# GpSimd's gathers for the expert tiles without their pacing wait, and one weight residual moved behind the first gather

## The chip, the cores and the metric

The kernel runs on one core of a Trainium2 chip. The metric is the device time of one execution in microseconds (us). The five engines are written as the profile writes them: PE is TensorE (PEld its weight loads), DVE is VectorE, ACT is ScalarE, POOL is GpSimd, SP is SyncE. Each engine runs its own list of instructions in order, and they meet only at semaphores; SP carries most of the DMA issues.

## The reference, cut to what matters

```python
# x: (128, 32, 128) f32; cond_8: (128, 8) router logits
# layer 0: x1 = x + ternary_ffn(layernorm(base + LoRA(x)))
# layer 1, the stage this document is about:
rw = jax.nn.softmax(router_logits.astype(jnp.float32), axis=-1)
w, sel = jax.lax.top_k(rw, TOP_K)                       # 2 of 8 experts for each sequence
dense_w = jnp.zeros((B, E), x.dtype).at[jnp.arange(B)[:, None], sel].add(w)
def _gemma_mlp(x, gate_w, up_w, down_w):
    g = jnp.einsum('bsh,hi->bsi', x, gate_w)
    u = jnp.einsum('bsh,hi->bsi', x, up_w)
    return jnp.einsum('bsi,ih->bsh', jax.nn.gelu(g, approximate=True) * u, down_w)
out = sum_e dense_w[:, e] * _gemma_mlp(x, skill_gate[e], skill_up[e], skill_down[e])
out = out + _gemma_mlp(x, shared_gate, shared_up, shared_down)
# then a second, quantised gated FFN on out, and the residual
```

Batch row b is one sequence of 32 steps with 128 features. Each sequence goes through two of eight experts (hidden width 512) and through one shared expert.

## The kernel before

**Tiles and units.** The router's choice gives 256 (sequence, expert) pairs. They are laid into 20 tiles, each of one expert: 14 narrow tiles of 12 sequences (384 columns) and 6 wide ones of 16 (512 columns). The order is narrow, narrow, wide, repeated, with two narrow tiles at the end (`TILES`, `size(i)`). PE works each tile in two units, so there are units 0 to 39. Unit s is 12 matmuls of gate and up (`ps<-xg,Wr`). Behind each unit PE does the six down matmuls of the unit before: four on the high halves (`ps<-Hh,WT`) and two on the low halves (`ps<-Hl,WT`).

**Split operands.** Each f32 operand is carried as a rounded high part and a residual: `WD` slot 0 and slot 1 for the down weights, `Hh` and `Hl` for the hidden values. A residual is a subtraction of two SBUF tensors, `low(...)`: L746 on DVE, L1545 on POOL.

**POOL around the change.** `down_low(k)` (k = 0 to 7) makes the residual of expert k's down weights and raises `k_wdl`. `fetch(i)` gathers tile i's sequences out of `XT` into `xg[:, i % 4]`, one copy for each sequence (CAST rows of L1626). It works in two parts, the first 8 sequences and the rest, each with a register load of the sequence numbers (a TENSOR_LOAD) ahead. Its last copy raises `k_xg`, for which PE waits ahead of unit 2i. `fetch(0)` also waits for `d_xt` 8, the eighth low half of `XT`. From i = 4 on a fetch waits for `p_eu` to reach 2(i-4)+2, that is for PE to have read tile i-4 out of the same buffer. From i = 2 on each of its parts also waits for `d_ehl`, which DVE raises once for each unit's `Hl`: for 2i-3 ahead of the first part and for 2i-2 ahead of the second.

**DVE around the change.** In its loop over s it does: eight or six scatters `C<-ps,Wt,C` of an earlier tile, a register load (`colI`), `Hl` of unit s-1, and `HbS` (gelu times up) of unit s, which frees PE's banks.

**SP around the change.** `load_tile(i, ...)` moves tile i's gate and up weights (1 MB) from `wscr` into `Wr[:, i % 3]`. The raw down weights `wdr` were staged in the bytes that become `Wr[:, 0]` and `Wr[:, 1]`. So `load_tile(0)` waits for `k_wdl` 4 and `load_tile(1)` for `k_wdl` 8. PE waits for the load ahead of unit 2i. ACT's `down_weights(0)`, which copies tile 0's down weights from `WD` to `WT`, waits for `k_wdl` 8 as well.

Of the kernel before, what the change touches and what calls it, by code (L numbers as in the profile page):

```python
# [49 lines left out]
def program(nc, x, cond, Wb, bb, As, Bs, fw, gamma, beta, sg, su, sd, hg, hu, hd, wg, wu, wd, out):  # L50
    ctx = ExitStack()
    with ctx:
# [14 lines left out]
        def sem(name):  # L67
            return ctx.enter_context(nc.semaphore(name))
# [154 lines left out]
        k_xg, p_eg, p_eu, a_eg, d_eh, a_ehh, d_ehl, p_ed, d_ey = (  # L223
           
            sem(n) for n in ("k_xg", "p_eg", "p_eu", "a_eg", "d_eh", "a_ehh", "d_ehl", "p_ed", "d_ey"))
# [53 lines left out]
        def cols(j):  # L279
            return slice(512 * j, 512 * j + 512)  # L280
# [20 lines left out]
        def size(i):  # L301

            return 16 if TILES[i] < 16 else 12
# [1234 lines left out]
        def _(e):  # L1538
            w = Waits(e)
# [4 lines left out]
            def low(o_, a, hi):  # L1544
                return e.tensor_tensor(o_, a, hi.bitcast(F32), SUB)  # L1545
# [22 lines left out]
            for n in range(12):  # L1568
                i = n - 2
# [23 lines left out]
            def down_low(k):  # L1593
                w.wait_ge(a_wdh, k + 1)
                low(WD[:, 1, cols(k)], wdr[:, k, :], WD[:, 0, cols(k)]).then_inc(k_wdl, 1)
# [14 lines left out]
            def fetch(i):  # L1610
                w.wait_ge(d_ord, 1)
                w.wait_ge(a_q, 8)
                w.wait_ge(p_q, 8)
                w.wait_ge(d_xt, 8)
                if i >= XR:
                    w.wait_ge(p_eu, 2 * (i - XR) + 2)
                for a_, b_ in ((0, 8), (8, size(i))):

                    if i >= 2:
                        w.wait_ge(d_ehl, 2 * i - 3 + (a_ > 0))  # L1620
                    t = PT * TILES[i] + a_
                    regs = nc.values_load_multi_w_load_instructions(
                        ordI[0:1, t:t + b_ - a_], engines=(mybir.EngineType.Pool,), min_val=0, max_val=127,
                        skip_runtime_bounds_check_because=WHY)[1]
                    for s in range(a_, b_):
                        last = e.tensor_copy(xg[:, i % XR, :, T * s:T * s + T].rearrange("p a t -> p a t"),  # L1626
                                             XT[:, :, :, bass.ds(regs[s - a_], 1)].rearrange("p a t o -> p a (t o)"))
                last.then_inc(k_xg, 1)

            for k in (4, 5, 6):  # L1630
                down_low(k)
            fetch(0)
            down_low(7)
            for i in range(1, NM):
                fetch(i)

# [18 lines left out]
            for n_, step in enumerate(POOL_ORDER):  # L1655
# [3 lines left out]
                k = POOLED.index(p) if p in POOLED else None  # L1659
# [143 lines left out]
```

## Time and profile before

| | |
|---|---|
| median of 3 runs | 400.34 us (400.22 to 400.65) |
| the profiled execution's own time | 400.22 us |
| its span in the trace | 398.5 us |
| PE busy | 346.2 us, 87% of the span |
| DVE busy | 330.8 us, 83% |
| ACT busy | 263.0 us, 66% |
| POOL busy | 223.4 us, 56% |
| expert stage, units 0 to 39 | from 89.1 to about 229.9 us |

The 1.7 us between the profiled execution's time and its span lie outside the trace. The busy shares are means over stages of different kind, so they don't say what bounds the expert stage. That is read from PE's idle gaps in that stage and from what ends each of them.

### The profile page before, as it was taken

The page shows a single profiled execution, that of the slowest core. Times are in us where ns is not written, and L with a number is a line of the kernel's source. Part 1 is how long each engine was busy: PE and PEld are TensorE (multiplying, and loading weights), DVE is VectorE, ACT ScalarE, POOL GpSimd, SP SyncE. Part 2 cuts the span into 40 slices and gives each one's busy share as a digit, 9 for nine tenths or more (in the row PEclk, how much of TensorE's full clock was granted, in tenths as well). Part 3 has the DMA queues.
Part 4 walks back from the last instruction along what each step waited for, and adds up shares of the span by engine and source line. Part 5 has one row for each costly group of instructions (what it writes and reads, how often), then busy time and mean ns, then how long its engine had stood idle before and what let it go on. Part 6 is the DMA issues. An engine that isn't in the chain of part 4 may idle for free.

```text
span 398.5 us, 6226 instructions
## 1 busy us (share of the span) xinstructions
PE 346.2 (87%) x1754; PEld 285.0 (72%) x1754; DVE 330.8 (83%) x700; ACT 263.0 (66%) x339; POOL 223.4 (56%) x400
## 2 busy tenths in 40 slices
PE   8979967999999999999999989999999971005997
PEld 7657744768898989989898977777677650003897
DVE  4588558975999999999999989765689899979894
ACT  3655687866576565666656544555467899999650
POOL 2656885897466473847465023222195568992462
PEclk9998999999999999999999999999999996555999
DMA  6998993955353443535332005100000000000022
GB/s 173 341 398 301 326 314 118 315 161 212 112 202 111 151 168 117 201 106 187 132 127 84 3 2 160 51 2 0 1 2 0 1 0 1 0 0 2 0 108 105
DMA packets 19850, 47.77 MB, mean 120 GB/s; under 512 B 2787, under 2 KB 8934, under 8 KB 17254
## 3 DMA queue, kind: packets, MB, share of 16 engines
q1 hardware_dynamic: 18342, 47.16, 33.8%
q10 hardware_dynamic: 1472, 0.20, 0.3%
q8 instruction: 14, 0.23, 0.2%
q14 instruction: 22, 0.18, 0.1%
HBM read 33.10 MB, written 12.58 MB: 115 GB/s over the span
## 4 chain that ended last, share of the span: by engine, by line
PE 59%; DVE 15%; POOL 8%; issue 6%; DMA 6%; ACT 5%; ACTq 0%; DVEq 0%; SPq 0%; POOLq 0%
PE ps L378 57%; DVE S L755 3%; DMA wscr<-wst 2%; POOL XCh L1542 2%; POOL wst L1545 2%; DMA wdr<-n_L_cond_skill_down_dram 2%; DVE O_i L752 1%; PE ps L375 1%; DMA bsr<-in_L_cond_Bs_dram 1%; DVE G L746 1%; ACT U L1307 1%; POOL C_i L1542 1%; ACT ps L1307 1%; DVE Hl L746 1%; DVE HbS L746 1%
## 5 line engine op out<-in xcount | busy, mean ns | idle before, releaser
L1626 POOL CAST xg<-XT 128x64 fp32r x264 | 81.3, 356 | 52.6 <-DVE Hl L746 25.5
L378 PE MATMUL ps<-xg,Wr 128*128 128x384 f32 (+1 forms) x480 | 98.6, 354 | 0.3 <-issue 0.3
L378 PEld LDWEIGHTS ps<-xg,Wr 128*128 128x128 f32 x480 | 85.8, 188 | 7.5 <-issue 0.6
L1307 ACT ACTIVATE Hh<-HbS 128x512 fp32r<-128x512 f32 (+2 forms) x72 | 56.5, 785 | 46.2 <-DVE HbS L746 45.9
L746 DVE TENSOR_TENSOR HbS<-Gb,ps 128x512 f32<-128x512 f32 (+2 forms) x72 | 63.2, 878 | 21.7 <-PE ps L378 18.6
L1307 ACT ACTIVATE Gb<-ps 128x512 f32<-128x512 f32 (+2 forms) x72 | 54.1, 751 | 30.5 <-PE ps L378 28.7
L746 DVE TENSOR_TENSOR Hl<-HbS,Hh 128x768 fp32r<-128x768 f32 (+2 forms) x57 | 55.2, 969 | 2.3 <-ACT Hh L1307 1.8
L752 DVE SCALAR_TENSOR_TENSOR C<-ps,Wt,C 128x32 f32 x264 | 52.4, 279 | 2.9 <-PE ps L378 2.6
L378 PE MATMUL ps<-XT,SHh 128*128 128x512 f32 x128 | 45.7, 398 | 0.8 <-DVE XT L746 0.4
L1545 POOL TENSOR_TENSOR Hl<-HbS,Hh 128x512 fp32r<-128x512 f32 x15 | 19.7, 1316 | 47.0 <-ACT Hh L1307 46.9
L1307 ACT ACTIVATE ps<-G,S 128x1024 int32<-128x1024 f32 (+1 forms) x29 | 35.6, 1250 | 6.7 <-DVE O_i L752 5.7
L378 PE MATMUL ps<-Hh,WT 128*128 128x384 f32 (+1 forms) x160 | 37.3, 355 | 0.0
L378 PEld LDWEIGHTS ps<-Hh,WT 128*128 128x128 f32 x160 | 29.0, 188 | 2.1
L378 PEld LDWEIGHTS ps<-XT,SHh 128*128 128x128 f32 x128 | 24.0, 188 | 6.2 <-issue 0.7
L755 DVE TENSOR_REDUCE S<-G 128x1 f32<-128x1024 f32 (+1 forms) x26 | 28.1, 1125 | 0.2
L378 PE MATMUL ps<-XT,SHl 128*128 128x512 f32 x64 | 25.0, 391 | 0.0
L1545 POOL TENSOR_TENSOR wst<-stg,wst 128x512 fp32r<-128x512 f32 x16 | 20.6, 1310 | 7.2 <-ACT wst L1307 7.2
L378 PE MATMUL ps<-Hh,SD 128*128 128x512 f32 x64 | 21.4, 416 | 2.7 <-DVE Hl L746 2.7
L378 PE MATMUL ps<-Hl,WT 128*128 128x384 f32 (+1 forms) x80 | 23.1, 370 | 0.2 <-DVE Hl L746 0.2
L378 PE MATMUL ps<-WFd,G 128*128 128x128 f32 x192 | 22.0, 276 | 0.5 <-POOL G L1542 0.4
L378 PEld LDWEIGHTS ps<-WFd,G 128*128 128x128 f32 x192 | 21.7, 192 | 1.1 <-issue 1.1
L1542 POOL TENSOR_SCALAR G<-O_i 128x1536 f32<-128x1536 int16 (+2 forms) x12 | 12.5, 1045 | 17.6 <-DVE O_i L752 17.5
(222 smaller groups left out, 675.7 us busy)
## 6 DMA issues: line engine op xcount, KB each, us to landing
Wr<-wscr SPq DMA_DIRECT2D x20, 1024.0 KB, 4.8
wscr<-wst SPq DMA_DIRECT2D x16, 512.0 KB, 5.9
stg<-n_L_cond_skill_gate_dram SPq DMA_DIRECT2D x8, 256.0 KB, 7.6
stg<-in_L_cond_skill_up_dram SPq DMA_DIRECT2D x8, 256.0 KB, 7.9
wdr<-n_L_cond_skill_down_dram SPq DMA_DIRECT2D x8, 256.0 KB, 5.8
xscr<-X SPq DMA_DIRECT2D x8, 256.0 KB, 6.1
X<-xscr SPq DMA_DIRECT2D x8, 256.0 KB, 4.3
out_dram<-X SPq DMA_DIRECT2D x7, 256.0 KB, 2.0
```

The source lines that it names most:

```text
L375: return e.transpose(o_, i_, identF[:, :])
L378: return e.matmul(o_, l, r, start=start, stop=stop, skip_group_check=True)
L746: return e.tensor_tensor(o_, a, b, op)
L752: return e.scalar_tensor_tensor(out=o_, in0=a, scalar=s, in1=b, op0=op0, op1=op1)
L755: return e.tensor_reduce(o_, i_, X, op, apply_absolute_value=absv)
L1307: return e.activation(o_, i_, func, **kw)
L1542: return e.tensor_scalar(o_, a, s1, s2, op0, op1)
L1545: return e.tensor_tensor(o_, a, hi.bitcast(F32), SUB)
L1626: last = e.tensor_copy(xg[:, i % XR, :, T * s:T * s + T].rearrange("p a t -> p a t"), XT[:, :, :, bass.ds(regs[s - a_], 1)].rearrange("p a ...
```

## The change

`fetch(i)` no longer waits for `d_ehl`; what it still waits for are the conditions on `XT`, and `p_eu` from tile 4 on. On POOL the residual `down_low(6)`, which stood ahead of `fetch(0)`, now stands behind it, together with `down_low(7)`. Nothing is added or dropped in computation.

```diff
                 for a_, b_ in ((0, 8), (8, size(i))):
-
-                    if i >= 2:
-                        w.wait_ge(d_ehl, 2 * i - 3 + (a_ > 0))
                     t = PT * TILES[i] + a_
...
-            for k in (4, 5, 6):
+            for k in (4, 5):
                 down_low(k)
             fetch(0)
-            down_low(7)
+            for k in (6, 7):
+                down_low(k)
             for i in range(1, NM):
                 fetch(i)
```

On POOL, at the start of the expert stage, before (each fetch begins with the TENSOR_LOAD of `ordI`; WD rows are `down_low`; the last two TENSOR_LOAD rows are the two parts of `fetch(2)`):

```order
L1545 TENSOR_TENSOR WD<-wdr,WD 128x512 [waits a_wdh] x3
L1622 TENSOR_LOAD ordI [waits p_q,d_xt,a_q,d_ord]
L1626 ISA
L1626 COPY xg<-XT 128x2x32
...
L1545 TENSOR_TENSOR WD<-wdr,WD 128x512 [waits a_wdh]
L1622 TENSOR_LOAD ordI
...
L1622 TENSOR_LOAD ordI [waits d_ehl]
...
L1622 TENSOR_LOAD ordI [waits d_ehl]
```

The same place after the change:

```order
L1545 TENSOR_TENSOR WD<-wdr,WD 128x512 [waits a_wdh] x2
L1619 TENSOR_LOAD ordI [waits p_q,d_xt,a_q,d_ord]
L1623 ISA
L1623 COPY xg<-XT 128x2x32
...
L1545 TENSOR_TENSOR WD<-wdr,WD 128x512 [waits a_wdh] x2
L1619 TENSOR_LOAD ordI
```

One WD row went from above the first gather to below it, so the eighth `k_wdl` now has two residuals between it and the end of `fetch(0)` where it had one. The waits for `d_ehl` are gone.

On SP nothing moved; the rows are shown since one of its waits is for those residuals (after; the second `k_wdl` wait is `load_tile(1)`'s):

```order
L1743 ISA [waits k_wdl]
L1743 DMA Wr<-wscr 128x2048
L1749 DMA xscr<-X_49 128x512 [waits d_x1] x2
L1736 TENSOR_LOAD etI
L1736 ISA x2
L1743 ISA [waits k_wdl]
L1743 DMA Wr<-wscr 128x2048
```

The first of the two waits is for the fourth residual, the second for the eighth.

## Rows read from the trace of the kernel before

**Rows 1.** The chain that ended last, 84 to 100 us: start, us, what.
```profile
89.13 5.86 PE ps L378 x30
94.99 0.27 issue
```
**Rows 2.** Timeline of PE's weight loads: start, us, then instruction, count and idle time before.
```profile
89.10 2.03 PEld L378 LDWEIGHTS ps<-xg,Wr 128*128 128x128 f32 x12 [0.41 <-POOL xg L1626]
...
94.37 0.30 PEld L378 LDWEIGHTS ps<-Hl,WT 128*128 128x128 f32 x2 [0.18 <-DVE Hl L746]
95.23 1.36 PEld L378 LDWEIGHTS ps<-xg,Wr 128*128 128x128 f32 x8 [0.56 <-issue]
```
**Rows 3.** Timeline of SP's DMA issues, 90 to 96 us.
```profile
90.38 3.96 SPq L1745 DMA_DIRECT2D Wr<-wscr  x2
```
**Rows 4.** The tile Wr, 90 to 100 us, then in the whole span.
```profile
DMA to landing us min/median/max: 4.8/4.9/4.9
...
DMA to landing us min/median/max: 4.7/4.8/6.2
```
**Rows 5.** Timeline of POOL, 60 to 96 us.
```profile
80.36 4.24 POOL L1545 TENSOR_TENSOR WD<-wdr,WD 128x512 fp32r<-128x512 f32 x3
85.13 3.83 POOL L1626 CAST xg<-XT 128x64 fp32r x12 [0.53 <-issue]
88.93 1.28 POOL L1545 TENSOR_TENSOR WD<-wdr,WD 128x512 fp32r<-128x512 f32 x1
90.15 2.92 POOL L1626 CAST xg<-XT 128x64 fp32r x12
```
**Rows 6.** Timeline of DVE at the start of the stage.
```profile
81.66 1.79 DVE L746 TENSOR_TENSOR Hl<-HbS,Hh 128x512 fp32r<-128x512 f32 x1
83.37 0.68 DVE L746 TENSOR_TENSOR XT<-ps,XT 128x512 fp32r<-128x512 f32 x1
84.57 0.68 DVE L746 TENSOR_TENSOR Hl<-HbS,Hh 128x512 fp32r<-128x512 f32 x1
93.36 0.96 DVE L746 TENSOR_TENSOR Hl<-HbS,Hh 128x768 fp32r<-128x768 f32 x1 [0.91 <-ACT Hh L1307]
96.28 1.10 DVE L746 TENSOR_TENSOR Hl<-HbS,Hh 128x768 fp32r<-128x768 f32 x1 [0.91 <-ACT Hh L1307]
```
**Rows 7.** Timeline of POOL: the first copies of fetch(2), the first after a wait.
```profile
95.08 2.70 POOL L1626 CAST xg<-XT 128x64 fp32r x8 [2.01 <-DVE Hl L746]
```
**Rows 8.** Timeline of ACT, 90 to 93.5 us.
```profile
91.16 1.05 ACT L1307 ACTIVATE WT<-WD 128x1024 fp32r x1
```
**Rows 9.** Stretches of six units each: stretch, us, DVE busy (x), clock, DMA.
```profile
95.23:116.16 20.93, 18.07 (x45) 1.00 0.39 149
116.16:137.38 21.22, 19.82 (x53) 1.00 0.42 150
```
**Rows 10.** PE's weight loads in one later stretch of six units.
```profile
157.48 0.71 PEld L378 LDWEIGHTS ps<-Hh,WT 128*128 128x128 f32 x4
158.33 0.30 PEld L378 LDWEIGHTS ps<-Hl,WT 128*128 128x128 f32 x2
...
161.71 0.30 PEld L378 LDWEIGHTS ps<-Hl,WT 128*128 128x128 f32 x2 [0.30 <-DVE Hl L746]
```
**Rows 11.** Timeline of DVE in the same stretch.
```profile
149.38 1.23 DVE L746 TENSOR_TENSOR Hl<-HbS,Hh 128x1024 fp32r<-128x1024 f32 x1
...
153.18 1.30 DVE L746 TENSOR_TENSOR Hl<-HbS,Hh 128x1024 fp32r<-128x1024 f32 x1
...
157.31 0.96 DVE L746 TENSOR_TENSOR Hl<-HbS,Hh 128x768 fp32r<-128x768 f32 x1
```
**Rows 12.** Timeline of POOL in the same stretch.
```profile
154.99 1.02 POOL L1626 CAST xg<-XT 128x64 fp32r x4 [1.59 <-DVE Hl L746]
159.09 2.72 POOL L1626 CAST xg<-XT 128x64 fp32r x8 [3.08 <-DVE Hl L746]
```
**Rows 13.** PE's weight loads at the end of the stage.
```profile
229.90 0.19 PEld L378 LDWEIGHTS ps<-XT,SHh 128*128 128x128 f32 x1 [0.67 <-issue]
```

## The prediction

> **What bounds the kernel now.** I read the page's busy shares, then the chain that ended last, then PE's weight loads over the expert stage with what ended each idle time, and last what POOL, SP, ACT and DVE did just before those points. From unit 2 on the chain is PE almost without a break: one piece of 5.86 us ends at 94.99, a piece of 0.27 us named "issue" follows, and PE goes on at 95.26 [rows 1]. The start of the stage has two idle times in PE's weight loads that matter. Unit 0 starts at 89.10 after 0.41 us that ended with POOL's gather. Unit 2 starts at 95.23 after 0.56 us put down to "issue", so to nothing that the profile names [rows 2]. The second one can be named from the DMA: SP issued `load_tile(1)` at 90.38 [rows 3], and in this stretch such a load took 4.8 to 4.9 us to land [rows 4]. 90.38 + 4.8 = 95.18, and unit 2, the first of tile 1, starts 0.05 us later. So unit 2 waits for its weights. SP had in turn waited for the eighth residual: POOL ran it from 88.93 to 90.21 [rows 5], and SP's issue follows by 0.17 us.
>
> Later the stage repeats in stretches of six units (two wide, four narrow), 21.22 us each, the first one 20.93 us [rows 9]. PE loses only 0.30 us at 161.71 and, by 158.33 - (157.48 + 0.71), 0.14 us at 158.33, both for `Hl` from DVE [rows 10]. No row of the stage after unit 0 has PE waiting for POOL's gathers.
>
> **The residual that moves.** Before, POOL runs three residuals in 4.24 us from 80.36, so to 84.60, and the first copy of `fetch(0)` starts at 85.13 [rows 5]. Without the third residual POOL is free at about 83.2 (two thirds of 4.24). But `fetch(0)` needs the eighth low half of `XT`, which DVE finishes at 83.37 + 0.68 = 84.05 [rows 6]. From such a release to the first copy POOL needs 0.76 us: the `Hl` of 93.36 ends at 94.32, the copies behind its wait start at 95.08 [rows 6, 7]. So the first copy could start at 84.81, 0.32 us earlier than now. At that time DVE subtracts an `Hl` (84.57 to 85.25), and POOL's copies and DVE's two-operand subtractions hold each other up: 12 copies took 3.83 us here, with two such `Hl` among them, and 2.92 us at 90.15 with none [rows 5]. So I take the end of `fetch(0)` as unchanged at 88.9, and 0.32 us earlier as the other end. Even that end brings PE little: unit 0 had waited 0.41 us, and unit 2 waits for its weights in any case.
>
> Behind `fetch(0)` there are now two residuals instead of one. One takes 1.28 us, and what follows it starts 90.15 - 88.93 = 1.22 us after it [rows 5]. The eighth `k_wdl` comes 1.22 us later, at 91.4. Bounds: 0.32 less if `fetch(0)` ends early, so 0.9; and 0.5 more if a DVE `Hl` falls on them, since three residuals took 4.24 us where 3 x 1.25 = 3.75 are expected, so 1.7. No `Hl` lies between 88.9 and 91.5; the next is at 93.36 [rows 6]. I take 1.22.
>
> **Who waits for that.** SP first: `load_tile(1)` goes out at 91.6 and lands at 96.4; `load_tile(3)`, queued behind it on SP, is due only seven units ahead of its use. PE starts unit 2 at about 96.45 instead of 95.23, and nothing hides it: PE already stood there for 0.56 us [rows 2]. So **+1.22 us on the path**. ACT second: `WT<-WD` of tile 0 ran at 91.16 [rows 8] and can now start only at 91.45. That puts `Hh` and `Hl` of unit 0 some 0.3 us back at most, and PE's down matmuls of unit 0 end 0.3 us later; they stand ahead of unit 2 and are covered by its longer wait, so 0. Third, `fetch(1)`: its copies start at 91.4 instead of 90.15, take 2.92 us, and meet the `Hl` at 93.36, which costs them about 0.9. They end at 95.2, ahead of 96.45: 0, with 1.2 us of cover.
>
> **The wait that goes.** For tile i it held the first part until `Hl` of unit 2i-4, three units ahead of the need. Without it POOL gathers tiles 2 to 5 at once and then is held by `p_eu` alone, until PE has read tile i-4, some seven units ahead. Since PE never waited for these gathers, being earlier buys nothing: 0. What can change is which DVE instructions the copies run beside. An `Hl` of a wide unit took 1.23 us alone and 1.30 us when it met copies; the narrow ones took 0.96 alone and up to 1.10 [rows 6, 11]. The scatters and `HbS` don't change beside copies. Of the two `Hl` that PE waits for in a stretch, the one at 157.31 meets none (the copies end at 156.01), the next, which starts 1.62 us after those at 159.09 began, meets them [rows 11, 12]. After the change gathers start about 0.76 us behind the end of a tile's second unit: for the tile whose second unit is loaded by 155.31 + 2.18 = 157.5 that is 158.3, so the `Hl` at 157.31 stays free and the next one is met, as before. Sum of the wait: 0, with bounds of 0.1 us gained and 0.14 us lost for each of the two `Hl` in six stretches, so -1.2 and +1.7 us; I take 0, since the pattern at the two critical places is the same.
>
> On this the Trainium skill (SBUF — State Buffer, Who interferes with whom) speaks against the change: a VectorE instruction with two SBUF inputs and a GpSimd instruction that reads SBUF exclude each other for a whole instruction. The rows agree in kind (`Hl` took 1.79 us at 81.66 beside POOL's residuals, 0.68 at 84.57 [rows 6]), but for the copies they show at most 0.14 us. By the rule's full length, a copy at every critical `Hl`, it would be a rival's price, below.
>
> **Sum.** Profiled execution: 400.22 + 1.22 + 0 = 401.44 us. It lies 0.12 us under the median of 400.34, so the median after is 401.56, say **401.6 us**; by the bounds of the residual alone 401.2 to 402.1.
>
> **Rivals.**
> (1) *The later stretches give it back.* While PE waits for weights DVE and ACT run ahead. The first stretch, with DVE less loaded (18.07 against 19.82 us busy), took 20.93 us, the later ones 21.22 [rows 9]. If the lead carried through all five later stretches, each would save 0.29: 401.56 - 1.45 = 400.1 us. Against it: the 0.14 and 0.30 us come anew in each stretch behind the eight scatters of a wide tile, which start only when PE's down matmuls end. A chance of 0.10.
> (2) *The landing isn't what unit 2 waits for.* The profile calls the wait "issue", and there is another such wait of 0.67 us at 229.90 [rows 13] that no load explains. Then the change does nothing: 400.3 us. Against it: 0.05 us of agreement with the landing. 0.07.
> (3) *Faster than before.* Freed of its wait POOL stays clear of the critical `Hl`, and both of PE's waits in the five later stretches vanish: 5 x 0.44 = 2.2 us, so 401.56 - 2.2 = 399.4 us. It is on the faster side once it saves more than 1.22 us. Against it: the `Hl` at 157.31 met no copy and PE waited all the same. 0.05.
> (4) *More collisions.* The copies now meet the critical `Hl` each time, two in each of six stretches: 12 x 0.07 (1.30 - 1.23) = 0.8 us more, so 402.4 us. Were each held for a whole copy, 1.01 us / 4 or some 0.25 us [rows 12], it would be 12 x 0.25 = 3.0 and 404.6 us. 0.12 together, of which 0.02 for the latter. The latter is what the skill's rule named above would make of it; the 0.07 us in the rows speak against it.
>
> **How the numbers follow.** The forecast has 0.66. 0.2% of 400.3 is 0.8 us, about what a measurement can tell here, so faster means under 399.5 and slower over 401.1. Slower: 0.66 + 0.12 = 0.78. Within: 0.10 + 0.07 = 0.17. Faster: 0.05. The range takes in the forecast with its bounds, the first price of (4) and (2): 400.3 to 402.6 us; it leaves out (1) and (3) and the long form of (4), 0.17.
>
> **What the changed profile would show.** Right: two WD residuals behind the first 12 copies, ending near 91.4; the Wr load issued near 91.6; unit 2's first weight load near 96.45 with some 1.8 us idle before it; stretches of 21.2 us behind it; POOL's gathers released by PE and no more by DVE. Wrong: unit 2 still at 95.2 (rival 2); stretches of 20.9 (1) or 20.8 and less (3); stretches above 21.3 with `Hl` above 1.0 us at the two places where PE waits (4). A residual stretched by an `Hl`, or a load that lands in more than 4.9 us, up to the 6.2 us seen once elsewhere [rows 4], would shift unit 2 further.

## The result, and the profile after

| | before | after |
|---|---|---|
| median of 11 runs each on one chip | 400.31 us | 403.94 us |
| lowest to highest | 398.89 to 400.81 | 401.62 to 405.48 |
| ratio, with its 95% interval | | 1.0103 [1.0077, 1.0129] |
| profiled execution, and its span | 400.22, 398.5 | 404.97, 403.3 |

The change costs 1.03%, about 4.1 us. Slower was forecast, but by 1.2 us, and 403.94 lies outside the range of 400.3 to 402.6. Now and then an execution runs at a lower mean clock and takes over 1.5% longer than the fastest of its kernel; the ratios here and below leave such ones out, the medians don't.

The page of after names the loss already. These are three groups of instructions (busy us, mean ns of one | idle before them and what ended it):

```profile
L1623 POOL CAST xg<-XT 128x64 fp32r x264 | 80.4, 359 | 43.5 <-PE ps L378 41.2
...
L746 DVE TENSOR_TENSOR Hl<-HbS,Hh 128x768 fp32r<-128x768 f32 (+2 forms) x57 | 60.9, 1068 | 2.5 <-ACT Hh L1307 1.9
...
L378 PE MATMUL ps<-Hl,WT 128*128 128x384 f32 (+1 forms) x80 | 23.2, 372 | 4.8 <-DVE Hl L746 4.8
```

The gathers are now released by PE alone, as the change says. PE lost 4.8 us ahead of the matmuls that read `Hl`, all of it to DVE. In the summary of waits, PE's weight loads waited 13.4 us for `Hl` with 2.8 us as the longest, where the same line of before has 8.3 and 1.1 (us, count, longest):

```profile
PEld ps L378 <- DVE Hl L746: 13.4, 17, 2.8
```

To place it I cut the expert stage at the first weight load of units 0, 2, 8 and 39. Columns: stretch, us, then busy us and instructions of PE, PEld, DVE, ACT, POOL, the clock, the share and GB/s of the DMA. First before, then after:

```profile
89.10:95.23 6.13, 5.89 (x31) 5.03 (x30) 2.73 (x3) 3.91 (x5) 4.12 (x14) 1.00 0.55 179
95.23:116.16 20.93, 20.90 (x108) 19.26 (x108) 18.07 (x45) 13.67 (x15) 12.31 (x40) 1.00 0.39 149
116.16:226.06 109.90, 109.75 (x559) 99.28 (x559) 102.37 (x271) 69.60 (x78) 62.13 (x200) 1.00 0.37 135
```
```profile
88.79:96.62 7.83, 5.71 (x30) 4.96 (x30) 4.31 (x3) 3.91 (x5) 7.83 (x23) 1.00 0.54 199
96.62:120.41 23.79, 21.29 (x110) 19.22 (x109) 22.32 (x45) 13.20 (x15) 17.86 (x62) 1.00 0.29 112
120.41:230.25 109.84, 109.69 (x560) 99.35 (x559) 102.08 (x271) 69.66 (x78) 53.19 (x172) 1.00 0.38 135
```

Units 0 and 1 take 1.70 us more, the next six 2.86 us more, and the 31 units behind them the same as before (-0.06). That is 4.50 of the 4.8 us by which the spans differ. The granted clock is 1.00 in all of it, its upper level of 2.4 GHz, so the clock has no part in this. DVE has the same 45 instructions in the middle stretch and is busy for 4.25 us more (22.32 against 18.07).

PE's weight loads there (start, us, instruction, count, idle before and what ended it; they answer to [rows 2]):

```profile
96.34 0.30 PEld L378 LDWEIGHTS ps<-Hl,WT 128*128 128x128 f32 x2 [2.44 <-DVE Hl L746]
96.62 2.10 PEld L378 LDWEIGHTS ps<-xg,Wr 128*128 128x128 f32 x12
...
105.61 0.77 PEld L378 LDWEIGHTS ps<-Hh,WT 128*128 128x128 f32 x4
109.20 0.30 PEld L378 LDWEIGHTS ps<-Hl,WT 128*128 128x128 f32 x2 [2.82 <-DVE Hl L746]
```

The `Hl` rows of DVE, as [rows 6]:

```profile
93.17 3.12 DVE L746 TENSOR_TENSOR Hl<-HbS,Hh 128x768 fp32r<-128x768 f32 x1 [1.03 <-ACT Hh L1307]
...
98.25 1.15 DVE L746 TENSOR_TENSOR Hl<-HbS,Hh 128x768 fp32r<-128x768 f32 x1 [0.91 <-ACT Hh L1307]
...
101.47 0.95 DVE L746 TENSOR_TENSOR Hl<-HbS,Hh 128x768 fp32r<-128x768 f32 x1
...
104.47 4.68 DVE L746 TENSOR_TENSOR Hl<-HbS,Hh 128x768 fp32r<-128x768 f32 x1
...
111.59 1.23 DVE L746 TENSOR_TENSOR Hl<-HbS,Hh 128x1024 fp32r<-128x1024 f32 x1
```

And POOL, as [rows 5]:

```profile
84.83 3.82 POOL L1623 CAST xg<-XT 128x64 fp32r x12 [2.23 <-issue]
88.61 2.53 POOL L1545 TENSOR_TENSOR WD<-wdr,WD 128x512 fp32r<-128x512 f32 x2
91.08 19.41 POOL L1623 CAST xg<-XT 128x64 fp32r x68
113.34 3.94 POOL L1623 CAST xg<-XT 128x64 fp32r x12 [2.86 <-PE ps L378]
```

A narrow `Hl` alone takes 0.96 us. Two of the four narrow ones here took 3.12 and 4.68: 2.2 and 3.7 us of waiting. That they waited and did not merely run slowly can be seen on POOL. Its copies begin every 0.23 to 0.24 us all through such a time, and at the end of it one copy lasts for a whole `Hl`: 1.10 us at the end of both long waits. The copies of the run (min/median/max in ns):

```profile
L1623 POOL CAST xg<-XT x68: 288/297/1147, 91.1 to 110.2; 128x64 fp32r x68
```

Both long waits fall in one unbroken run of 68 copies, tiles 1 to 5, from 91.08 to 110.5. The `Hl` at 101.47 falls in the same run and waited for nothing. In the wait of 3.7 us about 15 copies went by. From 113 on the copies come in bursts of 12 and 16 with PE's release between them, and no `Hl` waits over 0.2 us again.

SP's load of tile 1's weights answers to [rows 3]:

```profile
91.32 2.71 SPq L1743 DMA_DIRECT2D Wr<-wscr  x2
```

It is issued 2.53 us behind unit 0's first load, where before it was 90.38 - 89.10 = 1.28. With 4.8 to 5.0 us to land it is there at 96.1 to 96.3. PE waited for the first long `Hl` until 96.34.

### The profile page after: what moved, and what is told of

It is laid out like the page before. It is cut to its first block, busy times and chain, and to the rows that moved or that the text cites. A ratio compares the mean times of both kernels' runs of the same rounds, so it can differ in the third digit from the quotient of the medians.

```text
span 403.3 us, 6210 instructions
## 1 busy us (share of the span) xinstructions
PE 348.9 (87%) x1754; PEld 287.4 (71%) x1754; DVE 337.5 (84%) x700; ACT 263.2 (65%) x339; POOL 222.0 (55%) x400
## 4 chain that ended last, share of the span: by engine, by line
PE 61%; DVE 14%; POOL 8%; issue 6%; ACT 5%; DMA 3%; SPq 1%; DVEq 1%; POOLq 1%; ACTq 0%
PE ps L378 59%; DVE Hl L746 3%; DVE S L755 3%; DMA wscr<-wst 2%; POOL XCh L1542 2%; PE ps L375 2%; DVE O_i L752 1%; DMA bsr<-in_L_cond_Bs_dram 1%; DVE C L752 1%; SPq L1704 1%; DVE G L746 1%; ACT U L1307 1%; POOL C_i L1542 1%; ACT ps L1307 1%; DVE HbS L746 1%
## 5 line engine op out<-in xcount | busy, mean ns | idle before, releaser
L1623 POOL CAST xg<-XT 128x64 fp32r x264 | 80.4, 359 | 43.5 <-PE ps L378 41.2
L746 DVE TENSOR_TENSOR Hl<-HbS,Hh 128x768 fp32r<-128x768 f32 (+2 forms) x57 | 60.9, 1068 | 2.5 <-ACT Hh L1307 1.9
```

The source lines that it names most:

```text
L746: return e.tensor_tensor(o_, a, b, op)
```

## The experiments

In the tables "stage" gives the us from unit 0 to unit 2, from unit 2 to unit 8 and from unit 8 to unit 39, in the profiled execution; before it is 6.13 / 20.93 / 109.90. An edit is shown against the kernel before, unless the text says otherwise. Kernels of one batch share their runs of the kernel before, whose medians were 399.95 us (e1 to e4), 400.05 (e5 to e8), 400.06 (e9 to e13), 400.24 (e14 to e17) and 401.54 (e18, e19). When a text below says that an `Hl` "waited", it is its time less 0.96 us (narrow) or 1.23 us (wide).

### The two parts apart

**e1, the waits removed and the order kept.**

```diff
-                    if i >= 2:
-                        w.wait_ge(d_ehl, 2 * i - 3 + (a_ > 0))
```

> The waits for d_ehl are gone, the residuals stand in the old order. Theory P (unbroken run of copies holds DVE off): 68 copies run without a pause from about 90.15 us, and one or more of the four Hl of units 0 to 3 last over 2 us where they took 1.0 to 1.1; nothing like it elsewhere; median 402 to 404 us, with a spread of 2 us or more between runs. Theory O (the moved residual is the cause, together with the late weights): 400.3 us, every Hl under 1.4 us.

Measured: 402.47 us, ratio 1.0071 [1.0048, 1.0095]; stage 6.25 / 23.12 / 109.80. POOL and the `Hl` that stood out:

```profile
89.50 23.41 POOL L1623 CAST xg<-XT 128x64 fp32r x80
```
```profile
106.33 4.00 DVE L746 TENSOR_TENSOR Hl<-HbS,Hh 128x1024 fp32r<-128x1024 f32 x1
```

A run of 80 copies, and an `Hl` of a wide unit waited 2.8 us. Removing the waits alone costs some 2.8 us by the ratio; in this profile units 2 to 7 take 2.2 us longer. Unit 0's `Hl` waited 0.7 us as well, but units 0 and 1 take only 0.12 us more.

**e2, the order changed and the waits kept.**

```diff
-            for k in (4, 5, 6):
+            for k in (4, 5):
                 down_low(k)
             fetch(0)
-            down_low(7)
+            for k in (6, 7):
+                down_low(k)
```

> The residual stands behind the first gather, the waits are kept. Theory P: unit 2's first weight load at 96.4 instead of 95.2, no long Hl, median 401.5 us. Theory O: the whole loss is here, 403 to 404 us. If the landing of the weights is not what unit 2 waits for: 400.3 us.

Measured: 401.04 us, ratio 1.0045 [1.0022, 1.0068]; stage 7.49 / 20.93 / 109.83. SP's issue, and PE's loads of units 0 and 2:

```profile
90.68 2.71 SPq L1746 DMA_DIRECT2D Wr<-wscr  x2
```
```profile
88.16 2.03 PEld L378 LDWEIGHTS ps<-xg,Wr 128*128 128x128 f32 x12 [0.41 <-POOL xg L1626]
...
95.64 1.36 PEld L378 LDWEIGHTS ps<-xg,Wr 128*128 128x128 f32 x8 [1.12 <-issue]
```

The issue stands 2.52 us behind unit 0 instead of 1.28, unit 2 follows it by 4.96 us, and "issue" is named again as what ended PE's idle time. Units 0 and 1 take 1.36 us longer. In this profile it is the step of 1.22 us in the forecast and nothing else: no `Hl` waited over 0.7 us. By the ratio e2 costs 1.8 us [0.9, 2.7]. The ratios of e1 and e2 give 2.8 + 1.8 us, against 4.1 us [3.1, 5.2] for the two together.

### Is it the start of the stage, or the long run?

**e3, the old order, with the waits kept for tiles 2 to 5 and gone from tile 6 on.** If the start of the stage made the loss, it should be gone.

```diff
-                    if i >= 2:
+                    if 2 <= i < 6:
                         w.wait_ge(d_ehl, 2 * i - 3 + (a_ > 0))
```

> Old order of the residuals, the waits are kept for tiles 2 to 5 and gone from tile 6 on. Theory P: gathers from tile 6 on come in bursts of at most 28 copies and then of 12 to 16, the time stays at 400.3 us and all Hl under 1.4 us. If the pacing matters in every stretch of six units: slower by 1 us or more, in stretches of more than 21.3 us.

Measured: 402.86 us, ratio 1.0087 [1.0052, 1.0121]; stage 6.13 / 20.90 / 112.15. The start is as before, and the loss has moved behind it:

```profile
119.37 18.10 POOL L1625 CAST xg<-XT 128x64 fp32r x60 [0.60 <-issue]
```
```profile
127.56 3.96 DVE L746 TENSOR_TENSOR Hl<-HbS,Hh 128x1024 fp32r<-128x1024 f32 x1
```

Where the waits stop, POOL catches up with the gathers that it may do in one run of 60 copies, and in it one `Hl` waited 2.7 us. So it is not the start's own state; the expectation missed.

**e4, gathers released in groups of three tiles from tile 8 on**, so that runs of 40 copies come up again and again.

```diff
-                if i >= XR:
+                if i >= 8:
+                    w.wait_ge(p_eu, 2 * (min(i - (i - 8) % 3 + 2, NM - 1) - XR) + 2)
+                elif i >= XR:
                     w.wait_ge(p_eu, 2 * (i - XR) + 2)
...
-                    if i >= 2:
+                    if 2 <= i < 8:
```

> Old order; tiles 2 to 7 as before, and from tile 8 on the gathers of three tiles are released together by one wait on PE, so 40 copies run without a pause once in each stretch of six units. Theory P: long Hl (over 2 us) come back in the middle of the stage, in one or more of the four bursts, and the time is 401.5 to 406 us. Rival D (the long Hl at the start come from the DMA traffic or the state of the start, not from the length of the run): no Hl over 1.5 us, 400.3 us.

Measured: 400.54 us, ratio 1.0019 [0.9994, 1.0043]; stage 6.34 / 20.93 / 109.84; no `Hl` in the runs waited over 0.12 us:

```profile
138.11 11.87 POOL L1628 CAST xg<-XT 128x64 fp32r x40 [2.56 <-PE ps L378]
159.36 12.02 POOL L1628 CAST xg<-XT 128x64 fp32r x40 [9.38 <-PE ps L378]
```
```profile
140.23 0.95 DVE L746 TENSOR_TENSOR Hl<-HbS,Hh 128x768 fp32r<-128x768 f32 x1
```

Either 40 copies are too short a run, or it matters which `Hl` the run meets: here these were the narrow ones only.

**e7, six buffers and groups of five tiles from tile 6 on**: longer runs, which meet wide units too.

```diff
-XR = 4
+XR = 6
...
-                if i >= XR:
+                if i >= 6:
+                    w.wait_ge(p_eu, 2 * (min(i - (i - 6) % 5 + 4, NM - 1) - XR) + 2)
+                elif i >= XR:
                     w.wait_ge(p_eu, 2 * (i - XR) + 2)
...
-                    if i >= 2:
+                    if 2 <= i < 6:
```

> Old order; six gather buffers instead of four; tiles 2 to 5 paced as before, from tile 6 on five tiles are released together by one wait on PE, so runs of about 68 copies come at three places in the middle of the stage. Theory P: of some twelve to fifteen Hl that meet these runs three or more last over 2 us, and the time is 402 to 408 us. Rival D (the length of the run is not what counts, since groups of three had no long Hl in their profile): no Hl over 1.5 us, 400.3 us.

Measured: 409.49 us, ratio 1.0260 [1.0194, 1.0325]; stage 6.17 / 20.90 / 119.43.

```profile
118.45 21.73 POOL L1628 CAST xg<-XT 128x64 fp32r x72 [0.60 <-issue]
161.53 20.75 POOL L1628 CAST xg<-XT 128x64 fp32r x68 [21.35 <-PE ps L378]
```
```profile
126.65 3.70 DVE L746 TENSOR_TENSOR Hl<-HbS,Hh 128x1024 fp32r<-128x1024 f32 x1
...
173.76 4.03 DVE L746 TENSOR_TENSOR Hl<-HbS,Hh 128x1024 fp32r<-128x1024 f32 x1
...
197.85 3.69 DVE L746 TENSOR_TENSOR Hl<-HbS,Hh 128x1024 fp32r<-128x1024 f32 x1
```

The effect can be made at will in the middle of the stage: three runs (the third of 52 copies), four waits of 2.5 to 2.8 us (and one of 0.7). The stage past unit 8 is 9.5 us longer.

**e18, groups of three with other members**, so that runs of 40 copies meet the wide units. The edit is against e4.

```diff
-                if i >= 8:
-                    w.wait_ge(p_eu, 2 * (min(i - (i - 8) % 3 + 2, NM - 1) - XR) + 2)
+                if i >= 6:
+                    w.wait_ge(p_eu, 2 * (min(i - (i - 6) % 3 + 2, NM - 1) - XR) + 2)
...
-                    if 2 <= i < 8:
+                    if 2 <= i < 6:
```

> Groups of three tiles again (runs of 40 copies, a deep queue), but shifted so that each run meets the Hl of a narrow unit and of both units of a wide tile, where the earlier grouping met narrow ones alone and had no long Hl. If what decides is which Hl meets the run (in the long runs so far, the Hl of over 2 us of waiting were those of wide units, 8 of 11): one or more wide Hl wait over 2 us here, 402 to 408 us. If a run must be longer than about 50 copies (rival L): none, 400.3 us.

Measured: 408.72 us, ratio 1.0150 [1.0075, 1.0225]; stage 6.13 / 20.90 / 118.48. Its profiled execution took 413.17 us at a mean clock of 0.929, so its time isn't used. In the expert stage its clock was 0.99 to 1.00, and the rows can be read:

```profile
149.80 11.40 POOL L1628 CAST xg<-XT 128x64 fp32r x40 [10.12 <-PE ps L378]
```
```profile
155.22 4.42 DVE L746 TENSOR_TENSOR Hl<-HbS,Hh 128x1024 fp32r<-128x1024 f32 x1
```

The run of 40 from 174.97 had another `Hl` of 3.08 us, the one from 197.67 one of 3.69, and a run of 48 one of 3.23: waits of 1.8 to 3.2 us, one in each run. So 40 copies are enough. What separated e4 from e18 is which `Hl` its runs met. It isn't simply the width: the two long waits of the changed kernel's profile were at narrow `Hl`. (The count in the expectation above, 8 of 11, should be 10 of 12 by the traces that were there.)

### What lets DVE in

**e5, gathers paced by PE one unit apart instead of by DVE.**

```diff
-                if i >= XR:
-                    w.wait_ge(p_eu, 2 * (i - XR) + 2)
+                if i >= 2:
+                    w.wait_ge(p_eu, 2 * i - 3)
...
-                    if i >= 2:
-                        w.wait_ge(d_ehl, 2 * i - 3 + (a_ > 0))
```

> Old order of the residuals, no wait for d_ehl, but from tile 2 on each gather waits until PE has read the first unit of the tile two back, so a gather is never part of a run of more than 16 copies. Theory P (a long unbroken run of copies holds DVE off): no Hl over 1.4 us, 400.0 us, as before. Rival W (what protected Hl was that copies began just behind one): Hl over 2 us appear here too, and the time is 401.5 us or more.

Measured: 402.54 us, ratio 1.0056 [1.0032, 1.0081]; stage 6.47 / 21.04 / 110.05 in a profiled execution of 401.89 us. Only the first `Hl` waited (0.9 us), in a first run of 28 copies. The stage of this profile is 0.6 us longer than before's, the ratio says 2.2 us. One profile doesn't show where the rest went, and it stays open.

**e11, each half of a gather paced by PE**: behind `fetch(1)` runs of at most 8 copies. They start within some 0.6 us of where they started before, and not the 2.3 us earlier that the expectation names.

```diff
                     if i >= 2:
-                        w.wait_ge(d_ehl, 2 * i - 3 + (a_ > 0))
+                        w.wait_ge(p_eu, 2 * i - 2 + (a_ > 0))
```

> Old order; in place of the waits for d_ehl each half of a gather waits for PE: the first half until PE has read the whole tile two back, the second one unit later. The copies then come 2.3 us earlier against DVE's subtractions than before, in runs of at most eight, with never more than five waiting in POOL's queue. If the depth of POOL's queue decides (theory Q): no Hl over 1.4 us, 400.0 us. If the copies must begin just behind an Hl (rival W): 401.5 us or more, with long Hl.

Measured: 400.33 us, ratio 0.9999 [0.9969, 1.0029]; stage 6.29 / 20.93 / 109.84; no `Hl` waited over 0.12 us. The wait for DVE isn't needed as such: this other wait, which keeps the runs short too, does the same. What copies do that begin at another point of DVE's work was not tried here.

**e6, the changed kernel with a 128x16 memset on POOL ahead of every fourth copy of tiles 0 to 5**: is an instruction that reads nothing from SBUF enough to let DVE in? The edit is against the changed kernel.

```diff
                     for s in range(a_, b_):
+                        if i < 6 and s % 4 == 2:
+                            e.memset(pause[:, 64 * i + 16 * (s // 4):64 * i + 16 * (s // 4) + 16], 0.0)
```

> The changed kernel with a memset of 128x16 between every four copies of tiles 0 to 5; the memset only writes. Theory P in the form that DVE gets in at the first instruction of POOL that doesn't read SBUF: no Hl of units 0 to 3 waits more than about four copies, 1.1 us, and the time falls from 403.9 to 401.5 us. Rival Q (the depth of POOL's queue decides, whatever is in it): the long Hl stay, 403 to 404 us.

Measured: 402.57 us, ratio 1.0065 [1.0029, 1.0101]; stage 7.46 / 23.41 / 109.86. Two long waits (1.4 and 2.9 us) stay:

```profile
92.44 2.34 DVE L747 TENSOR_TENSOR Hl<-HbS,Hh 128x768 fp32r<-128x768 f32 x1 [1.10 <-ACT Hh L1308]
...
110.99 4.15 DVE L747 TENSOR_TENSOR Hl<-HbS,Hh 128x1024 fp32r<-128x1024 f32 x1
```
```profile
92.83 0.10 POOL L1625 MEMSET pause<- 128x16 f32 x1
...
110.90 0.10 POOL L1625 MEMSET pause<- 128x16 f32 x1
110.95 4.33 POOL L1626 CAST xg<-XT 128x64 fp32r x14
```

These rows settle less than it seems. The longer wait, from 110.99 to 113.9, holds no memset at all: the last one, at 110.90, ended as that `Hl` began, and 14 copies stand behind it without one. It is this wait that makes the 23.41. The shorter wait passed over the memset at 92.83 and ended at 93.82, where the next one stood. So one memset did not let DVE in, and a second may have. The strict form of the theory, that DVE gets in at the first such instruction, has this one case against it. Whether memsets shorten a wait was not shown: they would have to stand behind tile 5 too.

**e12, the changed kernel with POOL's queue kept short.** In the trace POOL prepares the addresses of its copies well ahead of the copies themselves: at the start of the long waits 8 to 12 of them stood ready. Here every second copy first waits for the copies before it, so that at most three are in the queue, the running one included; copies and their number are the same. The edit is against the changed kernel.

```diff
                     for s in range(a_, b_):
+                        if s % 2 == 0:
+                            w.wait_ge(k_cp, copied[0])
                         last = e.tensor_copy(...)
+                        if s % 2 == 0:
+                            last.then_inc(k_cp, 1)
+                            copied[0] += 1
```

> The changed kernel; ahead of every second copy POOL waits for the copy before the last one to be done, so that no more than three copies are queued, while the run of 68 copies stays as long. Theory Q (DVE is held off while eight or more reading instructions are queued on POOL): no Hl over 1.5 us, unit 2 at +7.4 us from unit 0 from the late weights alone, 401.3 us. Rival L (the length of the run decides): long Hl stay, 403 to 404 us.

Measured: 402.17 us, ratio 1.0029 [1.0003, 1.0055]; stage 7.54 / 20.99 / 109.97.

```profile
92.73 8.21 POOL L1628 CAST xg<-XT 128x64 fp32r x28
101.21 3.68 POOL L1628 CAST xg<-XT 128x64 fp32r x12 [0.26 <-issue]
105.17 3.76 POOL L1628 CAST xg<-XT 128x64 fp32r x12 [0.29 <-issue]
```
```profile
94.81 1.02 DVE L747 TENSOR_TENSOR Hl<-HbS,Hh 128x768 fp32r<-128x768 f32 x1 [1.12 <-ACT Hh L1308]
...
109.54 1.29 DVE L747 TENSOR_TENSOR Hl<-HbS,Hh 128x1024 fp32r<-128x1024 f32 x1
```

The same copies at the same rate, but with a pause of 0.26 to 0.29 us at some of the loads of sequence numbers, and no `Hl` waited over 0.15 us. Units 2 to 7 are back at 20.99. What is left of the loss is the late weights: 7.54 against 6.13 us. The pauses cut the long run into runs of 8 to 28 copies, so a rival is open: that it is they, and not the short queue, that protect `Hl`. The run of 28 speaks against it. It met unit 0's `Hl` (94.81) with 8 copies gone and 19 to come, and that one waited 0.06 us; the same `Hl` waited 0.9 us in e5, in a run of 28 with the queue not limited, and 0.7 to 2.2 us in e1, e6, e13 and the changed kernel. One meeting is not proof.

**e15, e16, e19: groups of five (e7) with at most three, seven and five copies ready.** The edit is e12's on e7's kernel, with `copied[0] - 2` for seven and `copied[0] - 1` for five.

> Groups of five tiles as before (the variant with five Hl of over 0.5 us of waiting and 409.5 us), now with no more than three copies queued on POOL at any time. Theory Q (queue depth decides): the runs of copies stay at 50 to 68, no Hl waits more than 0.3 us, units 8 to 39 take 109.8 to 110.2 us as before the change instead of 119.4, median 400.3 us. Rival L (the length of the run decides): several long Hl, over 404 us.

> The same with up to seven copies queued. If any queue that stays short of about eight is harmless, as the profiles so far suggest (no Hl waited over 0.9 us with six or fewer queued): no long Hl, 400.3 us. If the risk grows with every queued copy: one or two Hl over 1 us of waiting, 401.5 to 405 us.

> Groups of five tiles with up to five copies queued; with seven there were three Hl of over 2 us of waiting (407.7 us), with three there was none (400.9 us). Rival L (only the length of the run and its breaks count): as with seven, 406 to 408 us. Theory Q in its second form (a bound between three and seven): either like three or like seven, which tells where the bound lies; I expect like seven, since before the change up to five were queued in runs of eight without loss only because such a run ends soon.

| | copies ready | us | ratio | stage |
|---|---|---|---|---|
| e7 | not limited | 409.49 | 1.0260 [1.0194, 1.0325] | 6.17 / 20.90 / 119.43 |
| e16 | seven | 407.74 | 1.0173 [1.0134, 1.0212] | 6.26 / 20.93 / 116.83 |
| e19 | five | 410.88 | 1.0233 [1.0164, 1.0303] | 6.08 / 20.94 / 116.98 |
| e15 | three | 400.88 | 1.0016 [0.9994, 1.0038] | 6.19 / 20.90 / 110.15 |

One `Hl` and one run of copies of e16, and of e19:

```profile
172.67 4.03 DVE L747 TENSOR_TENSOR Hl<-HbS,Hh 128x1024 fp32r<-128x1024 f32 x1
```
```profile
160.45 20.75 POOL L1633 CAST xg<-XT 128x64 fp32r x68 [19.23 <-PE ps L379]
```
```profile
131.23 4.35 DVE L747 TENSOR_TENSOR Hl<-HbS,Hh 128x1024 fp32r<-128x1024 f32 x1
```

With three, in e15, POOL's timeline breaks at each load of sequence numbers, and the longest of all 57 `Hl` (min/median/max ns) is the one at 82.0 us, behind POOL's residuals:

```profile
164.25 10.62 POOL L1633 CAST xg<-XT 128x64 fp32r x32 [0.26 <-issue]
```
```profile
L747 DVE TENSOR_TENSOR Hl<-HbS,Hh x57: 678/959/1798, 82.0 to 284.5; 128x768 fp32r<-128x768 f32 x28, 128x512 fp32r<-128x512 f32 x17, 128x1024 fp32r<-128x1024 f32 x12
```

So groups of five cost 9 us or nothing by the limit on the queue, with six buffers and the same order of gathers. Limits of seven and five leave most of the harm (the expectation of e16 had held seven harmless, if the queue stays short of eight); the limit of three takes it away. Two things change with that limit, though. Counted in the trace as prepared and not begun, the copies ready when an `Hl` began were at most five in e16, three in e19 and two in e12 and e15. And only e12 and e15 have the pauses of 0.26 us, which cut the runs to at most 32 copies, where e16 and e19 run 52 to 72 without one. Queue and pauses were not tried apart.

**e13, the changed kernel once more, a single run.**

> The changed kernel once more, for a second profile. Theory: the four Hl that meet the run of 68 copies are long in another pattern than in the first profile (there 2.16, 0.19, 0 and 3.72 us of waiting), all others stay under 0.2 us; unit 2 comes 7.4 to 7.9 us behind unit 0.

Measured: 403.23 us; stage 7.67 / 22.41 / 109.83. Two long waits again, but of 1.9 us at unit 0's `Hl` (93.98, 2.87 us) and 1.8 us at a wide one (108.97, 3.03 us), where the first profile of this kernel had 2.2 and 3.7 us, both at narrow ones.

The number of copies that pass an `Hl`, and partly which one they pass, changes between executions of the same program. The spread of the changed kernel, 3.9 us against 1.9 in 11 runs each, would fit this but shows little: in the batches of the experiments the kernel before spread over 3.2 to 5.4 us.

### The late weights

`load_tile(1)` must wait for the eighth residual only since the staged raw weights lie in the buffer that tile 1 gets. e8 (on e2's order) and e9 (on the kernel before) give tile 1 the third buffer, which is free early, and tile 2 the second, whose load then waits for the residual:

```diff
+        def WSLOT(i):
+            return (0, 2, 1)[i % 3]
...
-                if i in (0, 1):
-                    w.wait_ge(k_wdl, 4 * i + 4)
+                if i in (0, 2):
+                    w.wait_ge(k_wdl, 2 * i + 4)
...
-            load_tile(2, s_wr[2])
+            load_tile(1, s_wr[2])
...
-            load_tile(1, s_wr[1])
+            load_tile(2, s_wr[1])
```

> The moved residual with the waits kept, as in the run of the order alone, and in addition tile 1's weights are loaded early into the third weight buffer, while tile 2's take the second, which waits for the eighth residual. If unit 2 waited for its weights behind the residuals: its first weight load comes at 95.0 to 95.2 us, the loss of the order alone (1.1 us) is gone, median 399.7 to 400.0 us. If the order costs in another way: 401.0 us as before.

Measured: 400.61 us, ratio 1.0015 [0.9991, 1.0039]; stage 6.47 / 20.97 / 109.88. PE's loads:

```profile
94.47 0.30 PEld L382 LDWEIGHTS ps<-Hl,WT 128*128 128x128 f32 x2 [0.99 <-DVE Hl L750]
94.75 2.10 PEld L382 LDWEIGHTS ps<-xg,Wr 128*128 128x128 f32 x12
```

(PE's matmuls and its wait go by `WSLOT` too, which is left out above.) Unit 2 starts with no wait of its own. The 1.12 us named "issue" in e2 was the landing of the weights. What is left (0.3 us in the stage) is unit 0's `Hl`, which waited 0.7 us for `fetch(1)`'s copies.

> The kernel before, with tile 1's weights loaded early into the third buffer and tile 2's into the second behind the eighth residual. Unit 2 no longer waits for its weights: 5.9 us behind unit 0 instead of 6.13, median 399.7 us; a difference of 0.06% that the interval will not separate from none. If unit 2 waits for something else: 6.13 us as before.

> The kernel before with only the weight buffers exchanged, again, with more rounds: unit 2 comes 5.6 us behind unit 0 instead of 6.13. By that 0.5 us, 0.14% faster: median 0.5 us under the kernel before, interval perhaps just below 1. If the earlier 0.27% was luck of that chip: a ratio of 1.000.

Measured: 399.43 us, ratio 0.9973 [0.9946, 1.0001], and again 399.59 us, 0.9989 [0.9967, 1.0011]; stages 5.58 / 20.99 / 109.89 and 5.59 / 20.99 / 109.89. In both profiles units 0 and 1 take 0.55 us less than before, which is PE's wait of 0.56 us in [rows 2]. Neither interval keeps clear of 1, so no gain is claimed.

**e14.**

> The changed kernel with both cures: no more than three copies queued, and tile 1's weights in the third buffer. Theory: the two causes are the whole loss of 3.6 us, so the time is that of the kernel before, 399.6 to 400.4 us, with unit 2 6.0 to 6.5 us behind unit 0 and no long Hl. If something else of the change costs: over 401 us.

This text speaks of the changed kernel with both cures. The kernel that ran had both cures (the short queue of e12 and the buffers of e9) but was built on the kernel before: its waits for `d_ehl` and its order were still there. So the expectation was not tested. What ran shows that both cures together cost the kernel before nothing: 400.00 us, ratio 0.9987 [0.9967, 1.0007], stage 5.55 / 20.99 / 109.94. The changed kernel with both was not run.

## Why the prediction was right and wrong

**The residual that moves: right.** Two WD rows stand behind the first gather and end at 91.1 (91.4 forecast), and the load goes out at 91.32 (91.6). This whole profile is 0.3 us ahead of the one of before when the stage begins; behind unit 0's first load the issue stands 1.25 us later than before (1.22 forecast). The first gather came no earlier: its first copy begins 1.08 us behind the eighth low half of `XT`, after (84.83 against 83.07 + 0.68) as before (85.13 against 84.05). The 0.76 us that the prediction took for this from another release, and with it the earlier end of 84.81, did not come; it had rightly kept to the unchanged one. In e2, where this part stands alone, units 0 and 1 take 1.36 us longer, and e8 shows by another buffer that it was the landing. Rival 2 has fallen.

**The cover of `fetch(1)`: wrong in who waits.** The prediction saw its copies meet unit 0's `Hl` and said that this "costs them about 0.9". They went on, and `Hl` waited: 0.7 us in e2, 2.2 us in the profile of after. With the change in full, PE waited at unit 0's `Hl` until 96.34, up to 0.2 us beyond the landing, and unit 2 started 7.83 us behind unit 0, where the forecast has 96.45 - 89.10 = 7.35.

**The wait that goes: this step failed.** It was set at 0, with -1.2 to +1.7 us as bounds, "since the pattern at the two critical places is the same". That holds for the later stretches, which came out as before (109.84 against 109.90), and so rivals 1 and 3 have fallen. But the same paragraph says that "POOL gathers tiles 2 to 5 at once", and for that run it has no sum. The run was 68 copies, four `Hl` fell in it, and one of them cost PE 2.8 us, besides that of unit 0 above. e1 puts the term at 2.8 us [1.9, 3.8].

**The size of a meeting.** The bound was at most 0.14 us for one meeting, from `Hl` that had met bursts of 4 to 12 copies, and the long form of rival 4 had one whole copy, 0.25 us. Measured were up to 3.7 us, some 15 copies. The rows of before could not show it: no burst in it is long, and there are never more than five copies ready at an `Hl`. A safe bound for an unseen run would have been the run itself, by estimate 68 copies at 0.24 us, 16 us. Rival 4 had the mechanism (copies meet `Hl`) and the wrong place, length and count. The Trainium skill (SBUF — State Buffer, Who interferes with whom) had spoken against the change, and the kind of loss is the one it names: two SBUF inputs on VectorE against an SBUF read on GpSimd. Its size isn't: by that section of the Trainium skill whoever issues first has the ports for the whole instruction, which makes one copy of about 0.25 us, and the runs show a wait over some 8 to 15 copies. Here the measurement decides.

**What the cause is, and how far it is shown.** Shown: the loss of units 2 to 7 is DVE's `Hl` waiting while POOL's copies run. It goes with the waits (e1), follows the long run (e3, e7, e18), and disappears with the same copies when no more than three are in the queue (e12, e15). Whether the short queue does that, or the pauses that come with it, is not separated. Not settled either: why one `Hl` in such a run waits for 15 copies and its neighbour for none. Length of run alone isn't the answer (e4 against e18), and e6 leaves open what an instruction that reads nothing does between the copies. Most waits have one thing in common: of the 21 of 1.3 us and more in all profiles, 18 ended 0.4 to 1.8 us after PE had finished its last weight load and stood waiting for that very `Hl`. At 104.47 the wait ended at 109.15 - 0.96 = 108.2, and PE's last load at 105.61 + 0.77 = 106.4. But three (in e13, e16 and e18) ended within 0.1 us of PE's last load, so it is no rule. That PE's standing still lets DVE in isn't shown, since a long wait makes PE stand still in any case. A small shift of phase between copies and DVE is as good a guess.

## What to carry to other kernels

A wait that seems to make an engine early for nothing may be what keeps its runs short. Before it is removed, write down the longest run that the engine can then make, and which instructions of the engine that was seen to meet it fall into that run; if the trace shows only short bursts, their small cost is no bound for the long one. And when the run must stay, a wait on the engine's own last but one instruction, which keeps its queue short and puts in short pauses, cured it here (e12, e15), at no cost that could be measured (e14, e15), while a limit of five or seven instead of three left most of the loss.

## What the runs showed of the hardware that was not expected

- A subtraction of two SBUF tensors on DVE was passed by some 8 to 15 copies of POOL in a row, for 1.8 to 3.7 us (after, e1, e3, e7, e13, e16, e18, e19), while others in the same run waited 0 to 0.2 us.
- With at most three of POOL's copies in its queue none of the waits was over 0.16 us (e12, e15); with limits of five and seven they were up to 3.1 us (e19, e16). The pauses of 0.26 us in e12 and e15 may have a part in it.
- One memset of 0.10 us between the copies didn't let DVE in (e6, at 92.83, in a wait of 1.4 us).
- The profile named "issue" as what ended PE's wait for a DMA's landing (0.56 us before, 1.12 us in e2); moving the load away removed it (e8, e9).
